# The last feed-forward layer's matmuls in 64-row halves, two units as a pair, and transpositions beside the product with V

## The chip, the cores and the metric

The kernel runs on one core of a Trainium2 chip. The metric is the device time of one execution in microseconds. The kernel before takes 2092.36 us (median of 3 runs, 2091.86 to 2093.67).

## The reference

One transformer block over x of shape (8, 1024, 256), in float32, cut to what matters:

```python
qkv = (x @ w_qkv.T + b_qkv).reshape(b, n, 3, H, D).transpose(2, 0, 3, 1, 4)   # H = 16, D = 16
q, k = rope(elu(qkv[0]) + 1), rope(elu(qkv[1]) + 1)
attn = softmax(einsum('bhnd,bhmd->bhnm', q, k) / sqrt(D))
a = einsum('bhnm,bhmd->bhnd', attn, v)            # plus a depthwise convolution of v over 3 tokens
x = layernorm(x + a + lepe)
h = relu(s0 * concat(x, -x) @ W0) * 2             # W0: 512x1024, entries +1 and -1
h = relu(s1 * h @ W1) * 2                         # W1: 1024x1024
x = layernorm(x + s2 * h @ W2)                    # W2: 1024x256
```

## The kernel before, in words

**Steps.** The work is a row of 512 steps on one core: 8 batches, in each 8 pairs of heads, for each pair 8 steps, one for each tile of 128 keys (`kt` is the step's place in its pair). A batch has 64 steps; "step 26 of a batch" is its 27th. In each step TensorE (PE) makes four score tiles "S" (queries by keys, for the row maxima of a pair of heads 12 steps later; `scores`, L661), four transposed score tiles "T" (`scores_T`, L671), and the product of the step before's exponentials with V (`weighted_v`, L705: 16 fp32 matmuls, four at a time in 32 columns of the array each). S and T lie in different halves of the array's rows (48 and 50 of 64 rows), so one of each runs at the same time; that is called a pair here. VectorE (DVE) takes the row maxima of S (L1100), ScalarE (ACT) the exponentials of T (L923).

**Dense pieces.** The other matmuls are dealt to the steps as pieces (`dealt`, a table `DEALT[s]` written out by hand): the projections, transpositions of h, and the feed-forward layers L0, L1 and L2 of the batch before, in half batches of 512 tokens. An L1 unit is a 128x512 output; `in_pair` says that two L1 units go as a pair: each matmul takes 64 of the 128 contraction rows, one unit's matmul in the upper half of the array and the other unit's in the lower (`hidden_pair`, L821); the halves are then exchanged. A pair of units is four pieces, one for each of four steps. A step whose only piece is such a pair is `smooth`: its 16 matmuls are dealt in four quarters, one behind each S and T. In every other step the pieces stand in one block after the second S and T. An L2 unit (two tiles of 128 tokens by 256) is two pieces of 16 matmuls with all 128 rows and 256 columns (`ffn_out`, L835); a half batch has two units, so four pieces in four steps. There are 13 half batches whose L2 is dealt to steps (the last ones come after the loop), 52 pieces, of which 5 share their step with a `scale` piece. They stand in steps 54 to 57 and in 15 to 18 of the next batch (46 to 49 in the last batch).

**Transpositions.** At `kt` = 2 the attention rows of the pair of heads before are transposed (`o_rows`, four fp32 128x128 transpositions, L720; ACT copies them, L936; DVE takes the reciprocal one step later). At `kt` = 5 the row maxima of the next pair are transposed (`max_rows_T`, L713); DVE splits them in two (`split_max_rows`, L1121), and SyncE (SP) loads them into `q_stack` by four transfers (L575), which T of the next pair waits for at `kt` = 0. In every step both stand after the second S and T, ahead of the pieces.

**Banks.** S, T, the pieces and the transpositions share 7 PSUM banks. `Units` deals them ahead of time from one order, `program_order`, by estimated times; `wait_free` waits for the reader of a bank's last user. A pair of units holds two banks for four steps.

**First norm.** ACT normalises the rows of the first layer norm, two tiles a step (`NORMALISE_AT[0]`), with `ln_scale` from GpSimd (POOL).

Of the kernel before, what the change touches and what calls it, by code (L numbers as in the profile page):

```python
# [33 lines left out]
P = 128  # L34
# [39 lines left out]
MOMENTS_AT = {10: 0, 31: 1}  # L74
NORMALISE_AT = ({13: 0, 14: 2, 15: 4, 16: 6}, {37 + t: t for t in range(T)})
COPY_V_AT = {3: (0, 1, 2, 3, 4, 7), 1: (7,), 5: (7,)}
# [20 lines left out]
def in_pair(unit):  # L97


    return unit[0] == "L1" and unit[1] < NB - 1 and not (unit[1:3] == (NB - 2, 1) and unit[3] >= KF - 2)  # L100

# [107 lines left out]
def smooth(s):  # L209


    return len(DEALT[s]) == 1 and in_pair(DEALT[s][0][0])

# [24 lines left out]
def program_order():  # L238

    for u in START_UNITS:
        yield u, True, True, True
    for v in range(T + LEAD):
        if v == T + 1:
            yield ("max rows", 0), True, True, True
        for h in range(2):
            for half in range(2):
                yield ("S", v, h, half), True, True, True
    for s in range(STEPS):  # L250
        for u in pair_behind(s - 1)[:1]:
            yield u, False, False, True
        for i in range(4):
            h, half = divmod(i, 2)
            if s + T + LEAD < STEPS:
                yield ("S", s + T + LEAD, h, half), True, True, True
            yield ("T", s, 1 - h, half), True, True, True
            if i == 0:
                for u in pair_behind(s - 1)[1:]:
                    yield u, False, False, True  # L260
            if i == 1:
                if not pair_behind(s - 1):
                    for u in done_behind(s - 1):
                        yield u, False, False, True
                for u in own_units(s):
                    yield u, True, True, True
            for piece in DEALT[s] if i == 1 or smooth(s) else ():
                for q in (i,) if smooth(s) else range(4) if in_pair(piece[0]) else (None,):
                    for u in units_of(piece):
                        ends = ends_unit(piece) and q in (3, None)  # L270
                        yield u, piece[1] == 0 and q in (0, None), ends, ends and u not in done_behind(s)
        if s > 0:
            yield PV, False, False, False
    for u in done_behind(STEPS - 1):
        yield u, False, False, True
    for u in [("O rows", NB * PAIRS - 1), *END_UNITS]:
        yield u, True, True, True
# [90 lines left out]
def build(nc, x, xT, wT, b_qk, b_v, w_lepe, b_lepe, cos, sin, k0, k1, k2, s0, s1, s2, out):  # L368
    with ExitStack() as ctx:
# [285 lines left out]
        def _(pe):  # L655
# [105 lines left out]
            def input_bound(unit):  # L761
# [4 lines left out]
                                 ln_consts[:, 0, 3:4], start=True, stop=True).then_inc(units.full_sem(unit), 1)  # L766

            def transpose_h(unit):
                _, m, th, kc = unit
# [33 lines left out]
            def hidden_pair(first, second, part, quarters):  # L803
# [10 lines left out]
                for k in range(4 * ks + quarters[0], 4 * ks + quarters[-1] + 1):  # L814
                    if u == 0 and phase == 0:
                        units.wait_read(pe, ("L0", m, th, k))
                    for i in range(2):
                        for side in range(2):
# [5 lines left out]
                            if k == KF - 1 and i == 1:  # L824
                                done.then_inc(units.full_sem(unit) if phase == 1 else rows_crossed, 1)

            def ffn_out(unit, t):
                _, m, th, i = unit
# [9 lines left out]
                if t == 1:  # L838
                    done.then_inc(units.full_sem(unit), 1)

            def dense(unit, part):
                if unit[0] == "proj":
# [5 lines left out]
                elif unit[0] == "bound":  # L848
                    input_bound(unit)
                elif unit[0] == "hT":  # L850
                    transpose_h(unit)
                elif unit[0] == "L2":
                    ffn_out(unit, part)
                elif in_pair(unit):
                    hidden_pair(*units_of((unit, part)), part, range(4))
                else:
                    hidden(unit, part)
# [20 lines left out]
            for s in range(STEPS):  # L878
# [4 lines left out]
                for i in range(4):  # L883
                    score_tiles(s, *divmod(i, 2))
                    if i == 1:
                        for unit in own_units(s):
                            if unit[0] == "O rows":
                                o_rows(unit)
                            else:
                                max_rows_T(unit)  # L890
                        if not smooth(s):
                            for unit, part in DEALT[s]:
                                dense(unit, part)
                        if s > 0 and not DEALT[s]:
# [3 lines left out]
                    if smooth(s):  # L898
                        piece = DEALT[s][0]
                        hidden_pair(*units_of(piece), piece[1], (i,))  # L900
                if s > 0 and DEALT[s]:
# [12 lines left out]
        def _(act):  # L914
# [119 lines left out]
            for s in range(STEPS):  # L1034
# [4 lines left out]
                for unit in done_behind(s - 1):  # L1039
                    if unit[0] == "proj":  # L1040
                        elu_inputs(unit)
                if kt == O_ROWS_STEP and n > 0:
                    copy_o_rows(n - 1)
# [11 lines left out]
                for half in range(2):  # L1055
                    exp_probs(s, 0, half)
                for unit in done_behind(s):
                    if unit[0] in HIDDEN:
# [30 lines left out]
        def _(dve):  # L1089
# [247 lines left out]
            for s in range(STEPS):  # L1337
# [11 lines left out]
                if not pair_behind(s - 1):  # L1349
                    for unit in done_behind(s - 1):  # L1350
                        dense(unit)
                for unit in own_units(s):
                    if unit[0] == "max rows":
# [320 lines left out]
```

## Time and profile before

| | |
|---|---|
| median of 3 runs | 2092.36 us |
| profiled execution | 2091.6 us, span 2089.4 us, mean granted clock 0.985 |
| one batch of 64 steps, three times in a row | 249.34, 249.34, 249.35 us |
| busy in such a batch | PE 246.75, DVE 206.3, ACT 188.5, POOL 134.9 us |

In the 40 slices of the page the granted clock of TensorE is 9 or more tenths everywhere but in the first two. Steady batches repeat to within 0.01 us. So one step of each kind, read in the timeline of PE, stands for all of its kind. A step's length is the time from the first S and T of one step to those of the next.

### The profile page before, as it was taken

How to read it: one execution, taken by the hardware profiler on the slowest of the kernel's cores; microseconds unless marked ns; L12 is line 12 of the kernel's file. 1: busy time of each engine (PE TensorE's matmuls, PEld its weight loads, DVE VectorE, ACT ScalarE, POOL GpSimd, SP SyncE). 2: the span in 40 equal slices, each digit the busy share in tenths (PEclk: the TensorE clock that was granted, in tenths of full speed). 3: DMA queues.
4: the chain of work that ended last, by engine and by line, in shares of the span. 5: the costliest groups of instructions: out<-in, count | busy, mean ns of one | idle time of the engine just before them, and what ended most of it. 6: DMA issues, size and time to landing. Idle time of an engine off the chain costs nothing.

```text
span 2089.4 us, 47276 instructions
## 1 busy us (share of the span) xinstructions
PE 2031.0 (97%) x18910; PEld 845.3 (40%) x18910; DVE 1684.0 (81%) x3094; ACT 1519.8 (73%) x2867; POOL 1013.0 (48%) x583
## 2 busy tenths in 40 slices
PE   5999999999999999999999999999999999999998
PEld 3133323444434444344443443444443444444355
DVE  8989988788787988888787887878888788888243
ACT  3399888766877678876787767787687777877742
POOL 2958287614757067462584427752385603400110
PEclk7699999999999999999999999999999999999999
DMA  5001210020010200121000200002001020000000
GB/s 199 20 17 47 72 24 30 17 79 12 17 37 30 82 17 11 35 77 40 11 26 27 86 26 17 29 17 97 14 17 37 19 72 17 13 13 29 2 21 21
DMA packets 40443, 77.10 MB, mean 37 GB/s; under 512 B 15024, under 2 KB 19488, under 8 KB 37280
## 3 DMA queue, kind: packets, MB, share of 16 engines
q1 hardware_dynamic: 34496, 49.97, 8.4%
q0 software_dynamic: 5184, 23.07, 3.0%
q8 instruction: 149, 2.44, 0.5%
q10 hardware_dynamic: 544, 1.05, 0.1%
q14 instruction: 70, 0.57, 0.1%
HBM read 46.27 MB, written 25.17 MB: 34 GB/s over the span
## 4 chain that ended last, share of the span: by engine, by line
PE 82%; DVE 9%; ACT 6%; issue 2%; DMA 0%; SPq 0%; POOL 0%; POOLq 0%; ACTq 0%
PE o_bank L705 21%; PE unit_banks L821 17%; PE unit_banks L661 16%; PE unit_banks L796 8%; PE unit_banks L671 6%; DVE maxima L1100 6%; PE unit_banks L835 5%; PE unit_banks L732 5%; ACT probs L923 4%; PE unit_banks L720 2%; DVE hT L1169 1%; PE unit_banks L713 1%; DMA lepe_rows<-in_b_v 0%; ACT rows L1011 0%; DVE rows L1229 0%
## 5 line engine op out<-in xcount | busy, mean ns | idle before, releaser
L1100 DVE TENSOR_REDUCE maxima<-unit_banks 128x1 f32<-128x512 f32 x2048 | 1312.6, 683 | 258.7 <-PE unit_banks L661 257.3
L923 ACT ACTIVATE probs<-unit_banks 128x512 f32<-128x512 f32 x2048 | 1144.3, 605 | 446.6 <-PE unit_banks L671 423.0
L671 PE MATMUL unit_banks<-q_stack,k_stack 50*128 50x512 f16 x2048 | 698.1, 382 | 10.6 <-ACT probs L923 6.4
L661 PE MATMUL unit_banks<-k_stack,q_stack 48*128 48x512 f16 x2048 | 699.5, 387 | 4.8 <-DVE maxima L1100 3.1
L705 PE MATMUL o_bank<-probs,v_pair 128*32 128x256 f32 x8192 | 565.4, 387 | 4.0 <-issue 4.0
L821 PE MATMUL unit_banks<-h0T,w 64*128 64x512 f16 x3520 | 527.4, 376 | 0.2
L1513 POOL TENSOR_TENSOR attn<-o_rows_sb,rden 128x256 f32<-128x256 f32 x63 | 39.2, 622 | 747.1 <-DVE rden L1113 739.4
L705 PEld LDWEIGHTS o_bank<-probs,v_pair 128*32 128x32 f32 x8192 | 207.0, 109 | 306.4 <-issue 140.2
L661 PEld LDWEIGHTS unit_banks<-k_stack,q_stack 48*128 48x128 f16 x2048 | 153.1, 94 | 404.3 <-issue 199.7
L821 PEld LDWEIGHTS unit_banks<-h0T,w 64*128 64x128 f16 x3520 | 172.4, 95 | 156.0 <-issue 6.5
L671 PEld LDWEIGHTS unit_banks<-q_stack,k_stack 50*128 50x128 f16 x2048 | 156.0, 93 | 79.2 <-ACT probs L923 35.4
L1172 DVE SCALAR_TENSOR_TENSOR h1T<-unit_banks,h1T 128x512 f16<-128x512 f32 x128 | 87.4, 685 | 102.0 <-ACT h1T L987 102.0
L835 PE MATMUL unit_banks<-w,h1T 128*128 128x256 f16 x1024 | 121.4, 273 | 0.1
L796 PE MATMUL unit_banks<-hT,w 128*128 128x512 f16 x512 | 120.5, 380 | 0.8 <-DVE hT L1169 0.8
L1531 POOL TENSOR_TENSOR rows<-rows,lepe_tmp 128x1024 f32<-128x1024 f32 x48 | 113.5, 2365 | 3.8
L1529 POOL TENSOR_TENSOR lepe_tmp<-v_ext,lepe_rows 128x1024 f32<-128x1024 f32 x48 | 113.1, 2357 | 4.3 <-DVE max_rows L1121 1.7
L835 PEld LDWEIGHTS unit_banks<-w,h1T 128*128 128x128 f16 x1024 | 96.7, 98 | 28.9 <-issue 16.9
L987 ACT ACTIVATE h1T<-unit_banks 128x512 f16<-128x512 f32 x128 | 70.6, 605 | 48.8 <-PE unit_banks L796 48.8
L1545 POOL TENSOR_TENSOR neg_mean<-moments,ln_consts 128x8 f32<-128x8 f32 (+2 forms) x19 | 4.0, 209 | 206.6 <-DVE moments L1252 206.5
L732 PE MATMUL unit_banks<-xT_sb,wT_sb 128*128 128x512 f16 (+1 forms) x368 | 96.4, 400 | 0.9 <-ACT probs L923 0.4
L1172 DVE SCALAR_TENSOR_TENSOR h0T<-unit_banks,h0T 128x512 f16<-128x512 f32 x128 | 85.9, 683 | 8.3 <-ACT h0T L987 8.3
L987 ACT ACTIVATE h0T<-unit_banks 128x512 f16<-128x512 f32 x128 | 77.5, 605 | 9.9 <-PE unit_banks L796 7.5
(153 smaller groups left out, 1765.0 us busy)
## 6 DMA issues: line engine op xcount, KB each, us to landing
rows<-in_x POOLq DMA_DIRECT2D x8, 1024.0 KB, 6.4
q_stack<-q_scratch SPq DMA_DIRECT2D x128, 64.0 KB, 2.0
k_stack<-k_scratch SPq DMA_DIRECT2D x128, 64.0 KB, 2.0
work<-in_xT SPq DMA_DIRECT2D x7, 1024.0 KB, 7.5
q_scratch<-parts POOLq DMA_DIRECT2D x14, 512.0 KB, 3.4
k_scratch<-parts POOLq DMA_DIRECT2D x14, 512.0 KB, 3.2
out<-rows SPq DMA_DIRECT2D x7, 1024.0 KB, 5.5
q_stack<-q_scratch SPq DMA_DIRECT2D x128, 32.0 KB, 1.9
```

The lines of the kernel that those rows point to most:

```text
L661: nc.tensor.matmul(units.out(unit), q_stack[row:row + STACK, r, t * P:(t + 1) * P], k_stack[row:row + STACK, r, half * 512:(half + 1) * 51 ...
L671: nc.tensor.matmul(units.out(unit), k_stack[row:end, r, kt * P:(kt + 1) * P], q_stack[row:end, r, half * 512:(half + 1) * 512], start=True ...
L705: done = nc.tensor.matmul(o, v_pair[:, n % RING, kt, h, :], p[:, :, parity, :], start=kt == 0 and half == 0, stop=kt == T - 1, skip_group_ ...
L732: done = nc.tensor.matmul(out, kept, moved, start=kc == 0 and i == 0, stop=kc == KC - 1 and i == len(terms) - 1)
L796: done = nc.tensor.matmul(units.out(unit), w, a, start=k == 0 and i == 0, stop=k == tiles - 1 and i == 1)
L821: done = nc.tensor.matmul(units.out(unit), w1[r, k, unit[3] * P:(unit[3] + 1) * P], h0T[r, i, k, :], start=phase == 0 and k == 0 and i == ...
L835: done = nc.tensor.matmul(units.out(unit)[:, t * C:(t + 1) * C], h1T[:, a, k, (2 * i + t) * P:(2 * i + t + 1) * P], w2[:, k, :], start=k = ...
L923: nc.scalar.activation(probs[:, 2 * (kt % 2) + h, half * 512:(half + 1) * 512], units.out(unit), ACT.Exp, scale=exp_regs[2 * (n % PAIRS) + ...
L987: done = nc.scalar.activation(dst[:, 0, unit[3], :], units.out(unit), ACT.Relu)
L1100: nc.vector.reduce_max(maxima[:, v // T % 2, h * T + t, half:half + 1], units.out(unit), AXIS_X)\
L1172: free(unit, nc.vector.scalar_tensor_tensor(dst[:, 1, u, :], s, 0.0, dst[:, 0, u, :], ALU.max, ALU.subtract))
L1531: ins = combine(base, base, lepe_tmp[:], ALU.add)
```

## The change

`in_pair` takes L2 units too (not the last half batches), a new `ffn_out_pair` makes them, and steps with an L2 pair alone become smooth. In smooth steps the transpositions move from behind the second S and T to the end, just ahead of the product with V; ACT copies the attention rows behind all four exponentials of that step, DVE splits the row maxima in the next step. The first norm's tiles are normalised in steps 14 to 17 instead of 13 to 16.

```diff
-NORMALISE_AT = ({13: 0, 14: 2, 15: 4, 16: 6}, {37 + t: t for t in range(T)})
+NORMALISE_AT = ({14: 0, 15: 2, 16: 4, 17: 6}, {37 + t: t for t in range(T)})
...
-    return unit[0] == "L1" and unit[1] < NB - 1 and not (unit[1:3] == (NB - 2, 1) and unit[3] >= KF - 2)
+    late = KF - 2 if unit[0] == "L1" else 0
+    return unit[0] in ("L1", "L2") and unit[1] < NB - 1 and not (unit[1:3] == (NB - 2, 1) and unit[3] >= late)
...
+            def transpose_rows(s):
+                for unit in own_units(s):
+                    if unit[0] == "O rows":
+                        o_rows(unit)
+                    else:
+                        max_rows_T(unit)
...
+            def ffn_out_pair(first, second, part, quarters):
+                _, m, th, _ = first
+                phase, t = divmod(part, 2)
+                if part == 0 and quarters[0] == 0:
+                    units.wait_free(pe, first)
+                    units.wait_free(pe, second)
+                    crossings[0] += 2
+                elif part == 2 and quarters[0] == 0:
+                    pe.wait_ge(rows_crossed, crossings[0])
+                for k in range(2 * quarters[0], 2 * quarters[-1] + 2):
+                    if part == 0:
+                        units.wait_read(pe, ("L1", m, th, k))
+                    for a in range(2):
+                        for side in range(2):
+                            unit = second if side != phase else first
+                            r = slice(ROWS * side, ROWS * (side + 1))
+                            col = (2 * unit[3] + t) * P
+                            done = nc.tensor.matmul(units.out(unit)[:, t * C:(t + 1) * C], h1T[r, a, k, col:col + P], w2[r, k, :],
+                                                    start=part == 0 and k == 0 and a == 0,
+                                                    stop=phase == 1 and k == KF - 1 and a == 1, skip_group_check=True)
+                            if t == 1 and k == KF - 1 and a == 1:
+                                done.then_inc(units.full_sem(unit) if phase == 1 else rows_crossed, 1)
...
-                    if i == 1:
-                        for unit in own_units(s):
-                            if unit[0] == "O rows":
-                                o_rows(unit)
-                            else:
-                                max_rows_T(unit)
-                        if not smooth(s):
-                            for unit, part in DEALT[s]:
-                                dense(unit, part)
+                    if i == 1 and not smooth(s):
+                        transpose_rows(s)
+                        for unit, part in DEALT[s]:
+                            dense(unit, part)
...
-                        piece = DEALT[s][0]
-                        hidden_pair(*units_of(piece), piece[1], (i,))
+                        dense_pair(DEALT[s][0], (i,))
+                if smooth(s):
+                    transpose_rows(s)
                 if s > 0 and DEALT[s]:
                     weighted_v(s - 1, 0)
                     weighted_v(s - 1, 1)
...
-                if kt == O_ROWS_STEP and n > 0:
+                if kt == O_ROWS_STEP and n > 0 and not smooth(s):
                     copy_o_rows(n - 1)
...
                     exp_probs(s, 0, half)
+                if kt == O_ROWS_STEP and n > 0 and smooth(s):
+                    copy_o_rows(n - 1)
...
-                for unit in own_units(s):
+                for unit in [*(own_units(s - 1) if smooth(s - 1) else ()), *(() if smooth(s) else own_units(s))]:
                     if unit[0] == "max rows":
                         split_max_rows(unit[1])
```

`program_order` follows each of these moves, so the banks are dealt anew.

## Rows read from the trace of the kernel before

**Rows 1.** The page, part 1: busy time, share of the span, instructions.

```profile
PE 2031.0 (97%) x18910; PEld 845.3 (40%) x18910; DVE 1684.0 (81%) x3094; ACT 1519.8 (73%) x2867; POOL 1013.0 (48%) x583
```

**Rows 2.** The page, part 4: the chain that ended last, by engine.

```profile
PE 82%; DVE 9%; ACT 6%; issue 2%; DMA 0%; SPq 0%; POOL 0%; POOLq 0%; ACTq 0%
```

**Rows 3.** Timeline of PE, an L2 step: start, length (us), engine, line, operation.

```profile
714.01 0.39 PE L661 MATMUL unit_banks<-k_stack,q_stack 48*128 48x512 f16 x1
...
714.54 1.92 PE L835 MATMUL unit_banks<-w,h1T 128*128 128x256 f16 x16
716.40 0.39 PE L661 MATMUL unit_banks<-k_stack,q_stack 48*128 48x512 f16 x1
...
717.94 0.39 PE L661 MATMUL unit_banks<-k_stack,q_stack 48*128 48x512 f16 x1
```

**Rows 4.** Timeline of PE, a smooth L1 step without a transposition.

```profile
742.55 0.39 PE L661 MATMUL unit_banks<-k_stack,q_stack 48*128 48x512 f16 x1
...
742.77 0.60 PE L821 MATMUL unit_banks<-h0T,w 64*128 64x512 f16 x4
...
745.26 1.07 PE L705 MATMUL o_bank<-probs,v_pair 128*32 128x256 f32 x16
746.26 0.39 PE L661 MATMUL unit_banks<-k_stack,q_stack 48*128 48x512 f16 x1
```

**Rows 5.** Timeline of PE, attention rows transposed in the middle of a smooth step.

```profile
505.77 0.66 PE L720 MATMUL unit_banks<-ident,o_sb 128*128 128x128 f32 x4
506.35 0.61 PE L821 MATMUL unit_banks<-h0T,w 64*128 64x512 f16 x4
```

**Rows 6.** Timeline of PE, a step without pieces: transpositions directly ahead of V.

```profile
179.93 0.38 PE L661 MATMUL unit_banks<-k_stack,q_stack 48*128 48x512 f16 x1
...
180.24 0.66 PE L720 MATMUL unit_banks<-ident,o_sb 128*128 128x128 f32 x4
180.83 0.64 PE L705 MATMUL o_bank<-probs,v_pair 128*32 128x256 f32 x8
```

**Rows 7.** Timeline of PE, maxima transposed in the middle of a smooth step.

```profile
735.02 0.38 PE L671 MATMUL unit_banks<-q_stack,k_stack 50*128 50x512 f16 x1
735.33 0.28 PE L713 MATMUL unit_banks<-ident,max_both 128*16 128x128 f32 x1
735.54 0.61 PE L821 MATMUL unit_banks<-h0T,w 64*128 64x512 f16 x4
```

**Rows 8.** Timeline of PE, transpositions that wait: steps 29 and 26 of a batch.

```profile
610.19 0.27 PE L713 MATMUL unit_banks<-ident,max_both 128*16 128x128 f32 x1 [0.22 <-DVE maxima L1100]
598.34 0.63 PE L720 MATMUL unit_banks<-ident,o_sb 128*128 128x128 f32 x4 [0.22 <-DVE maxima L1100]
```

**Rows 9.** Timeline of PE, the first step of an L1 pair behind another pair.

```profile
739.05 0.38 PE L661 MATMUL unit_banks<-k_stack,q_stack 48*128 48x512 f16 x1
739.49 0.39 PE L671 MATMUL unit_banks<-q_stack,k_stack 50*128 50x512 f16 x1
```

**Rows 10.** Timelines of PE (step 14 of a batch) and ACT (end of step 13).

```profile
553.23 0.39 PE L671 MATMUL unit_banks<-q_stack,k_stack 50*128 50x512 f16 x1 [0.80 <-ACT probs L923]
549.65 0.60 ACT L1011 ACTIVATE rows<-rows,shift,rstd 128x256 f32<-128x256 f32 x1
```

**Rows 11.** Timelines of DVE and SP, steps 5 and 6; a transfer's landing (page, part 6).

```profile
522.27 0.68 DVE L1100 TENSOR_REDUCE maxima<-unit_banks 128x1 f32<-128x512 f32 x1
518.91 2.65 SPq L575 DMA_DIRECT2D q_stack<-max_rows  x4
q_stack<-q_scratch SPq DMA_DIRECT2D x128, 64.0 KB, 2.0
```

**Rows 12.** Timeline of all engines, start of the step of rows 4.

```profile
742.97 1.34 DVE L1100 TENSOR_REDUCE maxima<-unit_banks 128x1 f32<-128x512 f32 x2 [0.92 <-PE unit_banks L661]
743.00 1.25 ACT L923 ACTIVATE probs<-unit_banks 128x512 f32<-128x512 f32 x2 [1.16 <-PE unit_banks L671]
```

**Rows 13.** The page, part 5: weight loads of the paired L1 matmuls.

```profile
L821 PEld LDWEIGHTS unit_banks<-h0T,w 64*128 64x128 f16 x3520 | 172.4, 95 | 156.0 <-issue 6.5
```

More of the change, by code:

```diff
@@ L209, in smooth @@
 def smooth(s):
-    return len(DEALT[s]) == 1 and in_pair(DEALT[s][0][0])
+    return s >= 0 and len(DEALT[s]) == 1 and in_pair(DEALT[s][0][0])
 def pair_behind(s):
@@ L264, in program_order @@
                         yield u, False, False, True
-                for u in own_units(s):
+                for u in own_units(s - 1) if smooth(s - 1) else ():
+                    if u[0] == "max rows":
+                        yield u, False, False, True
+                for u in () if smooth(s) else own_units(s):
                     yield u, True, True, True
@@ L271, in program_order @@
                         yield u, piece[1] == 0 and q in (0, None), ends, ends and u not in done_behind(s)
+        for u in own_units(s) if smooth(s) else ():
+            yield u, True, True, u[0] == "O rows"
         if s > 0:
@@ L839, in ffn_out, with dense_pair @@
                     done.then_inc(units.full_sem(unit), 1)
+            def dense_pair(piece, quarters):
+                pair = hidden_pair if piece[0][0] == "L1" else ffn_out_pair
+                pair(*units_of(piece), piece[1], quarters)
             def dense(unit, part):
@@ L851, in dense @@
                     transpose_h(unit)
+                elif in_pair(unit):
+                    dense_pair((unit, part), range(4))
                 elif unit[0] == "L2":
                     ffn_out(unit, part)
-                elif in_pair(unit):
-                    hidden_pair(*units_of((unit, part)), part, range(4))
                 else:
```

## The prediction

> **What bounds the kernel now.** I read the page first: TensorE's matmuls are busy for 97% of the span [rows 1], and 82% of the chain that ended last is PE's, the rest DVE, ACT and a little issue [rows 2]. Then the windows, one batch each: they repeat exactly, so one step of each kind stands for all. Then the timeline of PE step by step. The reader is to see that no step of the feed-forward part is bound by anything but PE's own sequence of matmuls, with three kinds of holes in it: where the array changes between matmuls of 64 rows, of 128 rows and of 32 columns; where a bank comes free late; and where ACT has fallen behind. The change touches all three.
>
> **L2 as pairs.** An L2 step lasts 717.94 - 714.01 = 3.93 us [rows 3]. A smooth L1 step, the same number of columns in 64-row pairs, lasts 746.26 - 742.55 = 3.71 us [rows 4]. The difference can be seen in the rows: the L2 block takes 716.40 - 714.54 = 1.86 us for 16 matmuls, that is 0.109 for each and about 0.1 us more than the matmuls to come back to 64 rows, and about as much is lost on entering it. In the new form 32 matmuls of 64 rows and 256 columns run as 16 pairs. Nothing in the trace is such a matmul. From below: half of the 0.22 us of a 512-column pair [rows 4], 0.109, as the full matmuls of 256 columns have it; 16 of them take 1.75 us, as 8 pairs of 512 columns do, and the step takes 3.71. From above: two weight loads one behind the other, 2 x 0.095 [rows 13], 0.19 a pair, and 5.0 us a step. I take 0.110 a pair and 3.73 a step, near the lower end, for this reason: at the start of the step of rows 4 nothing can be loaded ahead, since the array comes from 32-column matmuls. S and T start together at 742.55, and their readers start at 742.97 and 743.00 [rows 12]. If T's load had waited for S's, ACT would be 0.09 behind DVE, not 0.03. So the loads of the two halves run together, and one load fits under a matmul of 256 columns, as the 0.109 of rows 3 shows.
>
> The Trainium skill, "TensorE: Matmul & The Clock Gate", section "LDWEIGHTS (loading the stationary operand)", gives a load as the number of columns divided by 1.2 GHz, whatever the rows: by it two loads in series would be an estimated 0.21 us a pair, 3.4 us instead of 1.75, and an L2 step of 5.4 us. "TensorEngine Tiling (Array Packing)", section "Key Properties", says on the other hand that different tiles can execute loads and matmuls in parallel; by it the step is 3.73. The 0.03 us above speaks for the second.
>
> Of the 52 pieces 47 are alone in their step. 41 of these have no transposition: 41 x (3.93 - 3.73) = 8.2 us less. Six stand in step 18 with the attention rows. The timeline shows that step at 4.41; it becomes 3.73 + 0.59 (next part) = 4.32: 6 x 0.09 = 0.5 less. The 5 that share a step with `scale` stay one block behind 128-row matmuls, with as many changes of the array as before: nothing.
>
> **Transpositions at the end of smooth steps.** From a 64-row pair to the first transposition is 735.33 - 735.02 = 0.31 us [rows 7], the same as 180.24 - 179.93 in a step without pieces [rows 6]. From the first of the four transpositions of attention rows to the next matmul is 506.35 - 505.77 = 0.58 where 64-row matmuls follow [rows 5] and 180.83 - 180.24 = 0.59 where the product with V follows [rows 6]. Without a transposition the last pair is followed by V after 0.31: ten pairs of 0.218 from 742.77 put the last at 744.95, and V starts at 745.26 [rows 4]. So in the middle the four cost 0.31 + 0.58 - 0.22 = 0.67 us and at the end 0.31 + 0.59 - 0.31 = 0.59, which is one change of the array, 0.08 to 0.10, less; I take 0.09. For the maxima it is 0.31 + 0.21 - 0.22 = 0.30 in the middle [rows 7] and, with the same 0.21 behind it, 0.21 at the end: again 0.09. By the table of pieces, 28 smooth L1 steps have attention rows and 40 have maxima.
>
> Some of them also wait for a bank in the middle: 0.22 us, for the reader of an S tile [rows 8]. At the end of the step three more quarters have passed, the banks of that step's S and T are read, and V needs no bank of these, so I count the wait as gone. In the step lengths of the timeline that kind is told by 4.31 instead of 4.02 for maxima and 4.66 for attention rows whose pair begins behind single units.
>
> - maxima without the wait: 29 x 0.09 = 2.6
> - maxima with it (steps 13 and 29): 11 x 0.31 = 3.4
> - attention rows in a step that follows a pair: 14 x 0.09 = 1.3
> - attention rows behind L0 units (step 26): 7 x 0.31 = 2.2
> - attention rows behind L2 (step 58, 50 in the last batch): 7. Here 0.31 is saved, but L2 is now a pair, and behind a pair T of the second quarter comes 739.49 - 739.05 = 0.44 late [rows 9], since four banks are held by pieces. L2's banks are read by DVE alone and the first of them while PE makes the product with V, so that this wait may not come: between +0.14 and -0.31, I take -0.08: 0.6.
>
> What the moved instructions wait for and hold up: ACT's copy now stands behind the last exponential, ahead of the high parts and of the next step's exponentials. It waits for two quarters' pairs and the transpositions, some 0.7 us, while PE does the product with V for 1.0 us (746.26 - 745.26 [rows 4]); then T of the next step is not late. DVE's split of the maxima stands behind two low parts and two row maxima of the next step: in the step that begins at 520.65 they would be through at 522.27 + 0.6 = 522.9 [rows 11]. The four transfers take SP 2.65 us and the last lands 2.0 us after its start [rows 11], so at about 523.5 + 2.0 + 2.0 = 527.5; now they start at 518.91. T of the next pair of heads starts at 527.9. It is hidden, with 0.4 us to spare, or 0.7 by the split's own shorter times; in the last batch, where two steps there last only 6.7 us, it may cost 0.3 twice. SP's loads of the next stacks stand behind these transfers and move 4 us later, with five steps in hand. I cost all this at nothing, and keep for the range that the maxima come 0.5 us late at each of some 20 pairs: 10 us.
>
> **First norm one step later.** In step 14 of batches 2 to 6, T stands 0.80 us for ACT [rows 10], which from 548 on works without a pause at the projection's two activations, two tiles of the norm, two high parts and the exponentials. One of these tiles is the row at 549.65; two leave step 13, and ACT starts the next 0.5 us after each, so 1.0 us of the backlog goes ahead of that wait. They come back in step 17, where ACT has little else. Between 0 (another wait takes its place) and 1.0; I take 0.7: 5 x 0.7 = 3.5 us less.
>
> **Sum.** 8.2 + 0.5 + 2.6 + 3.4 + 1.3 + 2.2 + 0.6 + 3.5 = 22.3 us less than the profiled execution's 2091.6 (span 2089.4 and 2.2 around it): 2069.3. The median of the runs lies 0.8 above the profiled execution, so I forecast 2070.1 us.
>
> **Rivals.**
>
> 1. The bank waits change their place instead of going. For it: 7 banks, and L2 now holds two for four steps where it held one for two. Then the 0.22s and the norm's 3.5 stay, each of the 13 L2 pairs pays 0.44 in its first step as L1 does [rows 9], and what remains is 8.7 + 0.09 x 68 = 14.8 less, 5.7 more: 2083.3 us with the 0.8. Against it: behind single units the first step of an L1 pair pays little (3.79 us in step 7 of a batch against 3.71 in the timeline), and of the 13 L2 pairs 7 follow single units and 6 a step without pieces.
>
> 2. Slower: the weight loads of the two halves don't run together, or not wholly. Place: the L2 pairs alone, since only they have 256 columns for two loads; in L1 two loads of 0.095 fit in 0.22 and show nothing. Price: 16 x (0.19 - 0.11) = 1.3 us in each of 52 steps, 67 us: 2137 us. It decides from 0.110 + 22.3 / 52 / 16 = 0.137 us a pair, or 68 ns a load in series. Against it the 0.03 of rows 12.
>
> 3. PE is not fed fast enough. An L1 step has 40 matmuls and as many loads in 3.71 us, 46 ns each; a step of L2 pairs has 56 of each, 33 ns each. The product with V gets 32 in 1.00 us [rows 4], 31 ns each, but may live on what had queued up. If 40 ns were the limit, a step would take 4.48 us and 52 of them 39 more: 2109 us.
>
> **Chances.** The forecast 0.68, rival 1 0.21, rival 2 0.05, rival 3 0.04, something unnamed that leaves no difference 0.02. A measurement of this kernel tells a difference from about 0.2%, 4 us. Faster: 0.68 + 0.21 = 0.89; same 0.02; slower 0.09. The range: below, the norm's full 1.0, no wait behind L2 (-0.31 in place of -0.08) and 3.71 for the pairs take 1.5 + 1.6 + 0.9, and other bank waits in first steps of pairs (0.44 each) may go as the banks are dealt anew, another 5: 2061. Above it reaches to rival 1: 2084.
>
> **What would show it.** In the profile after, an L2 step of 3.71 to 3.75 us with 64x256 matmuls whose pairs start 0.109 to 0.112 apart; V 0.59 us behind the first of four transpositions; smooth steps with maxima of 3.92 us; no idle time ahead of L713 and L720; step 14 under 3 us. Pairs 0.13 or more apart would make rival 2 or 3 right; an idle time of PE at `kt` = 0 that ends with `q_stack<-max_rows`, or DVE and ACT waits in the first step of L2 pairs, would show rival 1's kind. The forecast is wrong if the time is above 2084.

## Result and the profile after

The change made the kernel slower by a hair: 2095.36 us (median of 20 runs, 2092.81 to 2097.77) against 2092.05 us for the kernel before in the same series, a ratio of 1.0015 with a 95% interval of 1.0008 to 1.0021. The forecast was 2070.1 us. The profiled execution took 2096.16 us, span 2094.0. One execution of all that are reported here, one of experiment 9, ran at a far lower clock (2569.71 us, mean granted clock 0.715) and is left out of every time below.

The page of the kernel after, parts 1, 4 and 5 (busy time, the chain that ended last, and the two groups of the new L2 matmuls: busy us and mean ns of one):

```profile
PE 2022.1 (97%) x19742; PEld 859.6 (41%) x19742; DVE 1685.7 (81%) x3094; ACT 1523.9 (73%) x2867; POOL 1013.0 (48%) x583
...
PE 83%; DVE 8%; ACT 6%; issue 2%; DMA 0%; SPq 0%; POOL 0%; POOLq 0%; ACTq 0%
...
L859 PE MATMUL unit_banks<-w,h1T 64*128 64x256 f16 x1664 | 122.8, 268 | 0.3
...
L859 PEld LDWEIGHTS unit_banks<-w,h1T 64*128 64x128 f16 x1664 | 80.8, 94 | 30.7 <-issue 0.4
```

PE's busy time fell by 8.9 us [rows 1], yet the span grew by 4.6: the work got cheaper and PE stood more. The windows of two batches show by how much, the step lengths below where (stretch, length; busy us of PE, PEld, DVE, ACT and POOL with their instructions; granted clock, DMA share, GB/s):

```profile
747.75:998.75 251.00, 245.44 (x2536) 106.48 (x2532) 206.60 (x382) 189.12 (x356) 134.94 (x74) 1.00 0.12 36
998.75:1248.58 249.84, 245.36 (x2534) 106.45 (x2531) 206.58 (x382) 189.08 (x356) 134.94 (x74) 1.00 0.12 36
```

A batch takes 249.84 us where it took 249.35, with PE busy for 245.4 instead of 246.75, at full clock. The first window, batch 3, holds 1.2 us more: that is its step 15 in the table. Step by step, a steady batch (steps of the kernel after are taken from the first T to the first T; batches are counted from 0):

| steps of a batch | before | after | forecast |
|---|---|---|---|
| L2 alone: 54 to 57, 16, 17 | 3.93 | 3.73 | 3.73 |
| 18 (L2, attention rows) | 4.41 | 4.32 | 4.32 |
| 5, 37, 45, 61 (maxima) | 4.02 | 3.92 | 3.93 |
| 2, 42 (attention rows behind a pair) | 4.86, 4.86 | 4.76, 4.81 | 0.09 less |
| 26 (behind L0) | 4.66 | 4.30 | 4.35 |
| 58 (behind L2) | 4.66 | 4.30 | 4.58 |
| 13, 29 (maxima, had waited) | 4.31 | 4.48 | 4.00 |
| 14 (norm) | 3.40 | 2.60 | 0.7 less |
| 6, 30, 46 (behind late maxima) | 3.48 | 4.12, 4.11, 4.07 | 3.48 |
| 38, 62 (behind late maxima) | 4.17 | 5.05 | 4.17 |
| 15 | 4.75 | 4.75, but 5.90 and 5.57 in two batches | 4.75 |

The differences of this table without step 15, with 0.08 that step 7 gained, add up to +0.51, and the batch grew by 0.49. Almost the whole loss is in the steps *behind* late maxima: +3.6 us a batch; 31 such steps in the whole trace grew by over 0.3 us each, 22.8 us in all, as much as the whole forecast gain of 22.3.

What the cheap part looks like: timeline of PE after, an L2 step (compare [rows 3]).

```profile
970.20 0.39 PE L667 MATMUL unit_banks<-k_stack,q_stack 48*128 48x512 f16 x1
...
970.42 0.60 PE L859 MATMUL unit_banks<-w,h1T 64*128 64x256 f16 x8
970.86 0.38 PE L667 MATMUL unit_banks<-k_stack,q_stack 48*128 48x512 f16 x1
...
972.92 1.07 PE L711 MATMUL o_bank<-probs,v_pair 128*32 128x256 f32 x16
973.93 0.39 PE L667 MATMUL unit_banks<-k_stack,q_stack 48*128 48x512 f16 x1
```

Eight matmuls are four pairs, 970.86 - 970.42 = 0.44 us, 0.110 a pair; the step takes 3.73. Now the dear part: timeline of PE after, steps 61 and 62.

```profile
988.77 0.28 PE L719 MATMUL unit_banks<-ident,max_both 128*16 128x128 f32 x1
988.98 1.07 PE L711 MATMUL o_bank<-probs,v_pair 128*32 128x256 f32 x16
989.98 0.39 PE L667 MATMUL unit_banks<-k_stack,q_stack 48*128 48x512 f16 x1
...
990.21 0.60 PE L834 MATMUL unit_banks<-h0T,w 64*128 64x512 f16 x4
...
991.09 0.39 PE L667 MATMUL unit_banks<-k_stack,q_stack 48*128 48x512 f16 x1 [0.29 <-ACT probs L962]
...
993.28 0.39 PE L677 MATMUL unit_banks<-q_stack,k_stack 50*128 50x512 f16 x1 [0.25 <-ACT probs L962]
...
995.03 0.39 PE L667 MATMUL unit_banks<-k_stack,q_stack 48*128 48x512 f16 x1
```

The transposition is done at 988.77 + 0.28, about 1 us before the next step begins. Its reader on DVE, same stretch:

```profile
989.60 0.69 DVE L1213 SCALAR_TENSOR_TENSOR h1T<-unit_banks,h1T 128x512 f16<-128x512 f32 x1
990.40 0.69 DVE L1141 TENSOR_REDUCE maxima<-unit_banks 128x1 f32<-128x512 f32 x1
991.01 0.68 DVE L1213 SCALAR_TENSOR_TENSOR h1T<-unit_banks,h1T 128x512 f16<-128x512 f32 x1
991.61 0.68 DVE L1141 TENSOR_REDUCE maxima<-unit_banks 128x1 f32<-128x512 f32 x1
992.21 0.27 DVE L1162 TENSOR_SCALAR max_rows<-unit_banks 16x128 f16<-16x128 f32 x1
992.51 0.28 DVE L1164 SCALAR_TENSOR_TENSOR max_rows<-unit_banks,max_rows 16x128 f16<-16x128 f32 x1
```

The two splits (L1162, L1164) stand behind two low parts (L1213; DVE's reading of the two banks of the pair before) and two row maxima (L1141). One bank of seven is held until 992.8, some 3.7 us after PE was done with it, while the new pair holds two, and those of the pair before come free only with the two low parts. PE waits of 0.29, 0.25 and more follow.

The profile ends these waits with ACT, though DVE holds the bank. The deal of `Units` for this step says why. When the second S and T are due, at about 990.65, six of the seven banks are taken: the maxima's, the new pair's two, one of the pair before (its low part ends at 991.69), and those of this step's first S and T. One is free and two are wanted, so the second S is dealt the bank of this step's first T and goes at 991.09, as soon as ACT has read that one (990.44 + 0.60, see the line). In the kernel of experiment 7 the same S is dealt the bank of the maxima, and nothing waits.

```profile
990.44 0.60 ACT L962 ACTIVATE probs<-unit_banks 128x512 f32<-128x512 f32 x1 [0.39 <-PE unit_banks L677]
```

Not all of the 0.88 us is the count of banks, though. The third T waits until 992.20 for the bank of the second (read until 992.14), while one of the old pair's had been free since 991.69: it was kept for the last S by the deal's estimated times. How much a better deal would have saved was not measured.

In the steps of the other kind the same shows as one wait, and steps 29 and 15 have waits of their own (PE and SP's queue):

```profile
863.06 0.27 PE L719 MATMUL unit_banks<-ident,max_both 128*16 128x128 f32 x1 [0.50 <-ACT work L1004]
...
865.43 1.47 PE L738 MATMUL unit_banks<-xT_sb,wT_sb 128*128 128x512 f16 x6 [0.57 <-DVE maxima L1141]
...
810.79 0.39 PE L667 MATMUL unit_banks<-k_stack,q_stack 48*128 48x512 f16 x1 [1.08 <-DMA q_stack<-max_rows]
```

```profile
805.45 2.65 SPq L581 DMA_DIRECT2D q_stack<-max_rows  x4
808.63 1.10 SPq L563 DMA_DIRECT2D q_stack<-q_scratch  x1
```

### The profile page after: what moved, and what is told of

It is laid out like the page before. It is cut to its first block, busy times and chain, and to the rows that moved or that the text cites. A ratio compares the mean times of both kernels' runs of the same rounds, so it can differ in the third digit from the quotient of the medians.

```text
span 2094.0 us, 48940 instructions
## 1 busy us (share of the span) xinstructions
PE 2022.1 (97%) x19742; PEld 859.6 (41%) x19742; DVE 1685.7 (81%) x3094; ACT 1523.9 (73%) x2867; POOL 1013.0 (48%) x583
## 3 DMA queue, kind: packets, MB, share of 16 engines
q8 instruction: 156, 2.56, 0.5%
## 4 chain that ended last, share of the span: by engine, by line
PE 83%; DVE 8%; ACT 6%; issue 2%; DMA 0%; SPq 0%; POOL 0%; POOLq 0%; ACTq 0%
PE o_bank L711 22%; PE unit_banks L667 16%; PE unit_banks L834 16%; PE unit_banks L809 9%; PE unit_banks L677 7%; PE unit_banks L738 6%; DVE maxima L1141 5%; PE unit_banks L859 4%; ACT probs L962 4%; PE unit_banks L726 2%; PE unit_banks L873 1%; ACT work L1004 1%; ACT work L1003 1%; DVE hT L1210 1%; PE unit_banks L719 1%
## 5 line engine op out<-in xcount | busy, mean ns | idle before, releaser
L1141 DVE TENSOR_REDUCE maxima<-unit_banks 128x1 f32<-128x512 f32 x2048 | 1315.1, 682 | 258.5 <-PE unit_banks L667 254.1
L677 PE MATMUL unit_banks<-q_stack,k_stack 50*128 50x512 f16 x2048 | 714.4, 382 | 9.0 <-ACT probs L962 5.0
L667 PE MATMUL unit_banks<-k_stack,q_stack 48*128 48x512 f16 x2048 | 713.2, 387 | 10.2 <-ACT probs L962 4.9
L667 PEld LDWEIGHTS unit_banks<-k_stack,q_stack 48*128 48x128 f16 x2048 | 161.0, 94 | 420.0 <-issue 192.7
L834 PEld LDWEIGHTS unit_banks<-h0T,w 64*128 64x128 f16 x3520 | 177.0, 95 | 152.2 <-issue 2.0
L677 PEld LDWEIGHTS unit_banks<-q_stack,k_stack 50*128 50x128 f16 x2048 | 164.8, 93 | 72.3 <-ACT probs L962 42.7
L1213 DVE SCALAR_TENSOR_TENSOR h1T<-unit_banks,h1T 128x512 f16<-128x512 f32 x128 | 87.6, 686 | 107.7 <-ACT h1T L1026 107.7
L859 PE MATMUL unit_banks<-w,h1T 64*128 64x256 f16 x1664 | 122.8, 268 | 0.3
L859 PEld LDWEIGHTS unit_banks<-w,h1T 64*128 64x128 f16 x1664 | 80.8, 94 | 30.7 <-issue 0.4
L1213 DVE SCALAR_TENSOR_TENSOR h0T<-unit_banks,h0T 128x512 f16<-128x512 f32 x128 | 85.8, 682 | 8.4 <-ACT h0T L1026 8.4
```

What stands on the lines that cost most here:

```text
L667: nc.tensor.matmul(units.out(unit), q_stack[row:row + STACK, r, t * P:(t + 1) * P], k_stack[row:row + STACK, r, half * 512:(half + 1) * 51 ...
L677: nc.tensor.matmul(units.out(unit), k_stack[row:end, r, kt * P:(kt + 1) * P], q_stack[row:end, r, half * 512:(half + 1) * 512], start=True ...
L834: done = nc.tensor.matmul(units.out(unit), w1[r, k, unit[3] * P:(unit[3] + 1) * P], h0T[r, i, k, :], start=phase == 0 and k == 0 and i == ...
L859: done = nc.tensor.matmul(units.out(unit)[:, t * C:(t + 1) * C], h1T[r, a, k, col:col + P], w2[r, k, :], start=part == 0 and k == 0 and a ...
L1141: nc.vector.reduce_max(maxima[:, v // T % 2, h * T + t, half:half + 1], units.out(unit), AXIS_X)\
L1213: free(unit, nc.vector.scalar_tensor_tensor(dst[:, 1, u, :], s, 0.0, dst[:, 0, u, :], ALU.max, ALU.subtract))
```

## The experiments

All kernels below come from the kernel after. A set `LATE` says whose transpositions stand at the end of smooth steps ("O rows" are the attention rows), the rest stays behind the second S and T; `program_order` follows; in 7 to 11 a bank's read is also counted where its reader stands in that order. Batch lengths are of steady batches. Differences in us are taken from 2092.05; the ratio, with its 95% interval, is to the kernel before in the same series.

**1. Maxima back in the middle.**

```diff
+LATE = ("O rows",)
+def mid_units(s):
+    return [u for u in own_units(s) if not (smooth(s) and u[0] in LATE)]
+def late_units(s):
+    return [u for u in own_units(s) if smooth(s) and u[0] in LATE]
...
+                    if i == 1:
+                        transpose_rows(mid_units(s))
...
-                if smooth(s):
-                    transpose_rows(s)
+                transpose_rows(late_units(s))
...
-                for unit in [*(own_units(s - 1) if smooth(s - 1) else ()), *(() if smooth(s) else own_units(s))]:
+                for unit in late_units(s - 1) + mid_units(s):
```

> The changed kernel with one thing put back: in smooth steps the maxima are transposed in the middle of the step again and split in the same step; the attention rows stay at the end, L2 stays in pairs, the norm one step later. Theory A (what was gained is given back by the maxima alone: their bank is taken ahead of the product with V and read only behind two low parts and two row maxima of the next step, so the next step waits for banks, and the load of the maxima comes late for step 16): the steps behind maxima (6, 30, 38, 46, 62 of a batch) go back to 3.48, 3.48, 4.17, 3.49, 4.17 us, no wait for q_stack<-max_rows at step 16, the rest of the gains stays: a steady batch near 246.4 us, the median near 2073. Rival B (L2 pairs hold two banks, the banks dealt anew make the waits, wherever the maxima stand): steps 6, 30, 38, 62 stay above 4.1, 4.1, 5.0, 5.0 and the median stays near 2091. Rival C (the norm's new steps cost it): median above 2085.

2072.46 us, ratio to the kernel before 0.9907 (0.9892 to 0.9922). Steps 6 and 30 take 3.48 again, 38 and 62 4.17, a batch 246.63: 3.2 us less than after, for a move that was to gain 0.1 to 0.3 us a step. The whole miss hangs on the maxima. This kernel changes place and reading at once, so it doesn't tell the two apart; 7 and 8 do.

**2. L2 pairs alone**, norm and transpositions as before.

```diff
-NORMALISE_AT = ({14: 0, 15: 2, 16: 4, 17: 6}, {37 + t: t for t in range(T)})
+NORMALISE_AT = ({13: 0, 14: 2, 15: 4, 16: 6}, {37 + t: t for t in range(T)})
+LATE = ()
```

> The kernel before with L2 in pairs alone: transpositions in the middle, norm in its old steps. Theory A: 47 steps go from 3.93 to 3.73 and nothing else moves, 9.4 us less, 2083. Rival B: the steps behind the maxima get longer here too, by some 3 us a batch, and the median is at or above 2092.

2088.26 us, 0.9982 (0.9973 to 0.9991): 3.8 us less than before where 9 were expected. The L2 steps are 3.73 here too. What they lose is in step 15 (timeline of PE, one row from each of two batches):

```profile
1052.67 1.92 PE L872 MATMUL unit_banks<-w,h1T 64*128 64x256 f16 x32 [0.34 <-DVE maxima L1154]
...
1301.17 3.35 PE L872 MATMUL unit_banks<-w,h1T 64*128 64x256 f16 x32 [0.34 <-DVE maxima L1154]
```

There L2 stands behind `scale`, needs a second bank, and waits 0.34 us: the step grows by 0.40 (5.15 for 4.75), 2.0 us in five batches. In the second row the same 32 matmuls take 3.35 us; that is the clock (last section). So the pairs keep their own gain and pay a little at one place, a small piece of rival 1.

**3. Both transpositions late, without L2 pairs and with the old norm**: `LATE = ("O rows", "max rows")`, `in_pair` for L1 alone, `NORMALISE_AT` as in 2.

> The kernel before with both transpositions at the end of smooth steps alone: L2 with 128 rows, norm in its old steps. Theory A: the steps behind maxima get longer by 0.6 to 0.9 us each as in the changed kernel, 3.6 us a batch, the transpositions give back 1.3, a median near 2103. Rival B: without L2 pairs no such waits, the transpositions gain, 2086. If step 16 waits for q_stack<-max_rows here too, the late load does not depend on the norm.

2110.93 us, 1.0094 (1.0079 to 1.0110): 18.9 us slower than before, worse than the 11 expected, a batch 252.22 against 249.35. The loss needs no L2 pair. Step 16 does not wait for the transfers here: step 15 takes 4.94 in every steady batch.

**4. The kernel after with the old norm steps** (the `NORMALISE_AT` line of 2 alone).

> The changed kernel with the norm back in steps 13 to 16. Theory A: step 14 goes back to about 3.4 us, and the wait for q_stack<-max_rows at step 16 (1.1 us) shrinks by about as much, since the split comes later too only if ACT is late; the median within 3 us of 2095. Rival C: if the norm's move is what costs, the median falls below 2090.

A miss: 2107.61 us, 1.0068 (1.0054 to 1.0081), 12 us slower than after. Its profiled execution, at a mean clock of 0.987, took 2098.98 us, against 2096.16 of the kernel after. A batch takes 250.85, 1.0 more than after, which its steps 15 of batches 3 and 5 (5.03 and 5.07 for 5.90 and 5.57) give back in part; over the whole execution the norm is worth 2.8 us here. Of the other executions three had a mean clock of 0.982 and took 2107.6 to 2108.6, one had 0.984 and took 2101.93. So some 9 of the 12 us between the medians go with the clock and not with the steps (last section).

**5. The norm alone**: the kernel before with only the new `NORMALISE_AT` line.

> The kernel before with the first norm one step later alone. If the parts add: step 14 goes from 3.40 to 2.56 us in batches 2 to 6, batch 1 loses 0.6, 4.8 us less in all, 2087.3. If the norm's gain needed the L2 pairs or the moved transpositions, the median stays at 2092.

2085.26 us, 0.9969 (0.9957 to 0.9980): 6.8 us less, more than the forecast's 3.5 and the 4.8 expected here. Step 14 takes 2.56 for 3.40, step 15 4.62 for 4.75, and batch 1 gains 1.55, of which the forecast had counted nothing.

**6. Maxima late alone**, split in the next step, nothing else changed: `LATE = ("max rows",)`, the rest as before.

> The kernel before with the maxima alone transposed at the end of smooth steps and split in the next step. Theory A: the whole loss is here. Steps 6, 30, 38, 46, 62 get 0.65, 0.63, 0.88, 0.57, 0.88 us longer, 13 and 29 0.17, steps 5, 37, 45, 61 0.10 shorter: a steady batch near 253.1 and a median near 2114. Rival B (needs L2 pairs or the attention rows at the end): below 2095.

2117.78 us, 1.0125 (1.0110 to 1.0141), 25.7 slower. Steps 6, 30, 46 take 4.12, 4.11, 4.07 and 38 and 62 5.05, as in the kernel after; steady batches take 253.10 but for batch 3, where the clock fell (last section). The cause is within this one part.

**7. Late transposition, but DVE's splits as the last work of the same step.**

```diff
-        for u in own_units(s) if smooth(s) else ():
-            yield u, True, True, u[0] == "O rows"
+        for u in late_units(s):
+            yield u, True, True, True
...
-                for unit in [*(own_units(s - 1) if smooth(s - 1) else ()), *(() if smooth(s) else own_units(s))]:
+                for unit in mid_units(s):
...
+                for unit in late_units(s):
+                    if unit[0] == "max rows":
+                        split_max_rows(unit[1])
```

> The changed kernel, maxima still transposed at the end of smooth steps, but DVE splits them as its last work of the same step, ahead of the low parts of the pair behind (the counts of reads follow the new order). Theory A1 (what costs is that the bank is read late): the waits behind the maxima go, the steps with maxima stay at 3.92, and the median comes to that of the kernel with the maxima in the middle less 0.09 x 40, 2069. Theory A2 (what costs is the place ahead of the product with V, where the transposition takes one more bank while a pair is read): the steps behind stay 0.5 us and more longer, the median above 2085.

2070.37 us, 0.9896 (0.9881 to 0.9911). The place is that of the kernel after; only the reader moved. Timelines of PE and of DVE, the same steps as above:

```profile
978.34 0.28 PE L731 MATMUL unit_banks<-ident,max_both 128*16 128x128 f32 x1
978.55 1.07 PE L723 MATMUL o_bank<-probs,v_pair 128*32 128x256 f32 x16
979.55 0.39 PE L679 MATMUL unit_banks<-k_stack,q_stack 48*128 48x512 f16 x1
...
980.66 0.39 PE L689 MATMUL unit_banks<-q_stack,k_stack 50*128 50x512 f16 x1
...
983.72 0.39 PE L679 MATMUL unit_banks<-k_stack,q_stack 48*128 48x512 f16 x1
```

```profile
979.16 0.27 DVE L1174 TENSOR_SCALAR max_rows<-unit_banks 16x128 f16<-16x128 f32 x1
979.47 0.28 DVE L1176 SCALAR_TENSOR_TENSOR max_rows<-unit_banks,max_rows 16x128 f16<-16x128 f32 x1
979.67 0.67 DVE L1225 SCALAR_TENSOR_TENSOR h1T<-unit_banks,h1T 128x512 f16<-128x512 f32 x1
```

The splits begin 0.8 us after the transposition does (3.4 us in the kernel after), the low parts come behind them, and step 62 takes 983.72 - 979.55 = 4.17 again. A batch:

```profile
738.97:985.34 246.37, 244.22 (x2534) 106.90 (x2532) 206.65 (x383) 188.88 (x357) 134.93 (x74) 1.00 0.12 37
```

**8. Transposition in the middle, split in the next step**: the fourth corner.

```diff
-                    yield u, True, True, True
+                    yield u, True, True, not (smooth(s) and u[0] == "max rows")
...
+                for unit in (own_units(s - 1) if smooth(s - 1) else []) + (mid_units(s) if not smooth(s) else []):
```

> The other half: maxima transposed in the middle of the step, split in the next step behind two low parts and two row maxima, attention rows at the end, L2 pairs, new norm steps. Theory A1: the waits come back though PE's order is that of the faster kernel, steps 6, 30, 38, 46 and 62 get 0.5 us and more longer, median 2090 or more. Theory A2: they don't, and the median is near 2072.

2102.43 us, 1.0049 (1.0034 to 1.0065). Steps 6, 30, 46 take 4.12, 4.11, 4.06 and 38 and 62 5.05: with the old place and the late reader the loss is all there. Timeline of PE and then of DVE:

```profile
989.50 0.28 PE L734 MATMUL unit_banks<-ident,max_both 128*16 128x128 f32 x1
...
993.66 0.39 PE L682 MATMUL unit_banks<-k_stack,q_stack 48*128 48x512 f16 x1 [0.29 <-ACT probs L977]
...
995.85 0.39 PE L692 MATMUL unit_banks<-q_stack,k_stack 50*128 50x512 f16 x1 [0.25 <-ACT probs L977]
```

```profile
994.78 0.27 DVE L1177 TENSOR_SCALAR max_rows<-unit_banks 16x128 f16<-16x128 f32 x1
```

With 1, 7 and the kernel after this makes a table, in us:

| | split in the same step | split in the next step |
|---|---|---|
| transposed in the middle | 2072.46 | 2102.43 |
| transposed at the end | 2070.37 | 2095.36 |

Across a row: 25 to 30 us. Down the left column, the move that the change was made of: 2.1 less. Down the right one 7.1 less: in 8, steps 13 and 29 take 4.94 for 4.48 after, 5 us over eleven steps, and the other steps with maxima take their 0.10 more.

**9. Late transposition, split in the next step, but as DVE's first work there.**

```diff
+        for u in late_units(s - 1):
+            if u[0] == "max rows":
+                yield u, False, False, True
...
+                for unit in late_units(s - 1):
+                    if unit[0] == "max rows":
+                        split_max_rows(unit[1])
```

(ahead of the low parts and the row maxima, on DVE and in the order by which the banks are dealt)

> The changed kernel, maxima transposed at the end, split by DVE first in the next step, ahead of the low parts instead of behind them and two row maxima. Theory A1 says the bank's read comes some 2 us earlier than in the changed kernel and near the one of the version split in the same step: steps 6, 30, 38, 46, 62 within 0.2 us of the kernel before, median 2070 to 2078. If the time depends on anything else that the late split moves (the transfers to q_stack alone), the waits ahead of S, T and pieces stay and the median is above 2088.

2071.56 us (three executions), 0.9903 (0.9883 to 0.9923), a batch 246.39, as in 7. It is not the boundary between the steps but what stands ahead of the reader.

**10. As 7, but steps 13 and 29, where a projection stands behind the step before, transpose in the middle.**

```diff
+    return [u for u in own_units(s) if smooth(s) and not (u[0] == "max rows" and proj_behind(s - 1))]
```

> The version split in the same step, but in steps 13 and 29, where a projection's bank is still being read by ACT, the maxima stay in the middle of the step. There the transposition waited 0.5 us for that bank: step 29 goes from 4.48 to 4.31, step 13 from 4.48 to 4.31 while step 14 gives 0.17 back. 1 us less than 2070.4: 2069.3; a rival, that the wait only moves, gives no difference.

2069.06 us, 0.9894 (0.9877 to 0.9910). Steps 13 and 29 take 4.31 instead of 4.48, a batch 246.20 instead of 246.37. The step lengths show it; the 1.3 us between the two medians alone would not.

**11. As 10, and L2's pair ahead of `scale` where they share a step.**

```diff
-        pieces.sort(key=lambda piece: piece[0][0] not in ("scale", "bound"))
+        pair = any(in_pair(piece[0]) for piece in pieces)
+        pieces.sort(key=lambda piece: (piece[0][0] not in ("scale", "bound")) != (pair and piece[0][0] == "scale" or pair and in_pair(piece[0])))
```

> As the one before, and where a scale piece shares a step with a pair (steps 15 and 40), the pair goes first. In step 15 the L2 pair waits for its second bank behind scale (step 15 is 5.02 us with pairs, 4.62 with 128-row L2). If the order is the cause, step 15 falls to 4.6 to 4.7 and step 40 by 0.1 (one change of the array less): 2 to 3 us less, 2067. If the banks are simply full, 5.0 stays and the median is within 1 us of the one before; the norm's and the split's later scale may cost POOL nothing or some us.

2068.66 us, 0.9887 (0.9870 to 0.9903), the fastest kernel measured, 23.4 us below the one before; against 10 no difference that can be told. Step 15 takes 4.96 instead of 5.03, step 40 stays at 4.35, and the pair still waits (timeline of PE):

```profile
1044.31 1.92 PE L877 MATMUL unit_banks<-w,h1T 64*128 64x256 f16 x32 [0.32 <-ACT probs L980]
```

The row names ACT, but ACT had read its bank by 1043.96, 0.35 us earlier. The pair's second bank is that of an S tile of the step before, which DVE reads until 1044.21, and when PE gets there (1043.99) the first is the only one of the seven that is free. So the banks are full at that point, whichever piece is dealt first.

**12. Attention rows late alone**: `LATE = ("O rows",)`, the rest as before.

> The kernel before with the attention rows alone at the end of smooth steps. The profile of the others says 0.36 us less in 14 steps (26, 58, 50) and 0.10 in 14: 6.4 us less, 2085.8. No rival wait is seen, since ACT copies them in the same step; if one comes it stands in steps 3, 27, 43, 59.

2088.54 us, 0.9983 (0.9973 to 0.9992): 3.5 us less than before where some 6 were expected. Steps 26 and 58 take 4.30, step 2 4.76, as after. In batches 4 and 6 of the profiled execution the clock fell (last section), which took 1.6 us back each time. ACT's copies, moved behind the exponentials, hold a bank too and cost nothing that shows: the steps behind them (3, 27, 43, 59) are as long as before.

## Why the prediction was wrong

**L2 as pairs: right.** 0.110 us a pair and 3.73 us a step were forecast, and both stand in the profile; in batches 2 to 6 the 35 steps 16 to 18 and 54 to 57 gave 6.4 us. Rival 2 (loads in series, 0.19 a pair) and rival 3 (a step of 4.48) are refuted by the same row. By the Trainium skill, "TensorE: Matmul & The Clock Gate", section "LDWEIGHTS (loading the stationary operand)", two loads one behind the other would be an estimated 0.21 us a pair; that the pairs are 0.110 us apart agrees with the Trainium skill, "TensorEngine Tiling (Array Packing)", section "Key Properties", by which tiles load and execute in parallel.

**The five steps with `scale`, "nothing": too low by 0.4 us each.** I counted changes of the array and not the second bank. It shows in experiment 2 as a wait of 0.34 and 5.15 for 4.75, and in experiments 1, 7 and 10 as 5.02 or 5.03 in step 15, where the new norm steps alone had made it 4.62 (experiment 5).

**Transpositions at the end: the size was right, 0.09 to 0.10** (5, 37, 45, 61, 2, 18). Behind L2 and L0 the wait went whole: 0.36 instead of 0.08 in step 58, 0.36 instead of 0.31 in step 26. Steps 13 and 29 failed: "V needs no bank of these, so I count the wait as gone". V doesn't, but the transposition itself does. At the end it was dealt the bank of the projection, which ACT reads at L1004, and waits 0.50: 11 x 0.17 us more, where 0.31 less was forecast.

**The norm: under-sized.** 0.80 to 0.84 instead of 0.70 in step 14 of a batch, 0.13 in step 15, and 1.55 in batch 1, which I had left out: 6.8 us in experiment 5.

**The step that failed is "What the moved instructions wait for and hold up", with its close "I cost all this at nothing".** It timed the split (at 522.9, 2.2 us into the step; the profile has 992.21 - 989.98 = 2.23) and asked only who waits for its *result*, the transfers and T of the next pair. It did not ask who waits for the bank that its *input* lies in. Just before it I had written that behind a pair "four banks are held by pieces" [rows 9]; with the maxima's bank that is five of seven, and S and T, two banks each time, have to make do with the other two. With the waits that the deal adds to it this costs 0.57 to 0.88 us in 31 steps, 22.8 us, and experiments 7 to 9 settle it: early reader 2070.4, 2071.6 and (experiment 1) 2072.5, late reader 2095.4 and 2102.4, wherever the transposition stands. Take that term out, and the kernel of experiment 7 lands at 2070.37 us beside the forecast 2070.1; the agreement is partly luck, since the norm gave some 3 us more and step 58 some 2, while steps 13 and 29 gave 5 less and step 15 some 2.

**Rival 1** named the kind (waits for banks that change place) but the wrong holder. Its 0.44 in the first step of a pair came, as 0.40, for the five pairs that begin in step 15, and not at all for those that begin in step 54 (3.73 us). My question about it was put to the new unit only, not to the moved transposition. No rival let the sign change through the banks.

**The transfers** were called hidden with 0.4 us to spare. Mostly they were, but twice, at the end of step 15 of batches 3 and 5, PE stood for them (1.08 us before 810.79, 0.75 in the other), the first time beside an issue of SP that took 1.10 us; 2.0 us in the whole trace. With the split in its own step the spare time is there again and nothing of it shows.

## What to carry over

For an instruction that is moved on an engine with buffers in common, ask two questions: who waits for what it writes, and who waits for what it reads to come free. Count the buffers held at the moment in question, with the reader's place in its own queue as the end of each, not the end of the writer. And when such a move costs, split it: the place of the writer and the place of the reader can be undone apart, and here only the second was bad.

## What the runs showed of the hardware

The granted clock of TensorE falls to its lower level for a part of step 15 in some batches and executions, and not in others that look the same before it. Windows of experiment 2, step 15 in batches 5 and 4 (columns as in the windows above):

```profile
1300.50:1304.50 4.00, 3.66 (x37) 3.03 (x39) 1.59 (x5) 1.54 (x4) 3.83 (x3) 0.57 0.11 29
1051.50:1055.50 4.00, 3.48 (x54) 2.78 (x56) 2.75 (x8) 2.67 (x7) 3.83 (x3) 1.00 0.20 44
```

The mean of 0.57 is 3.4 us at the lower level, 1.2 GHz, and the rest at the upper one. Pairs of 256 columns come 213 ns apart instead of 109, and the step takes 6.58 instead of 5.15 us, 1.4 us more. The same in experiment 12, step 15 of batch 4 (6.37 us for 4.75, 1.6 more), its lower level all the way:

```profile
1053.00:1056.40 3.40, 3.40 (x18) 2.04 (x17) 1.19 (x5) 1.14 (x3) 3.23 (x3) 0.50 0.06 19
```

In both kernels the step before has the old norm's 0.8 us in which PE stands [rows 10]. In batches 2 to 6 of the six profiled executions with that wait (the kernel before, experiments 2, 3, 4, 6 and 12) there are four such falls: one in 2, one in 6 (step 15 of batch 3, 6.56 us for 4.94) and two in 12. In the eight where step 14 is short (the kernel after, experiments 1, 5 and 7 to 11) there is none. But three of the six have none either, so what makes the clock fall is open.

The executions of experiment 4 differ by up to 10 us with mean clocks from 0.987 to 0.982. By an estimate from the falls above (3.4 us at half speed take 0.0008 off the mean clock of 2097 us, and cost 1.4 to 1.6 us), six falls would make both the 0.005 and 8 to 10 us; no trace of the slower ones was kept, so it stays an estimate. That moving the norm may be worth more than its 0.8 us a batch for this reason was not shown.
